# Attention operands turned by DMA instead of TensorE, and scores of two batches spread over two pairs of banks

## The chip, the cores and the metric

The kernel runs on one core of a Trainium2 chip. The core has TensorE (PE, matrix products and transposes into PSUM), VectorE (DVE), ScalarE (ACT), GpSimd (POOL) and SyncE (SP, which here only issues DMAs). Each engine works through its own list of instructions in order and waits on semaphores. The metric is device time in microseconds (us); three runs of the kernel before gave a median of 200.97 us (200.44 to 201.05). About 0.3% (0.6 us) is what such a measurement can tell from no change.

## The reference

The input x is 8 images of 16x16 positions with 128 channels, so 8 batches of 256 tokens. Three layers follow one another. Cut to what is computed:

```
# 1. self attention over positions (D = 16), all in float32
f, g, hh = xf @ Wf + bf, xf @ Wg + bg, xf @ Wh + bh
x = gamma * (softmax(f g^T) @ hh) @ Wv + bv + xf
# 2. t = t + attention_layer(layernorm(t)): 8 heads of 16
c = cos(h + theta); proj = cumprod(c) with column 0 = prod(c[1:])
ctx = softmax(proj proj^T / 4) @ proj          # queries = keys = values
x1 = layernorm(x + ctx @ W_comb.T + b_comb)
q = cos(x1[..., :8]) * cos(phi)
out = layernorm(x1 + relu(q @ W1.T + b1) @ W2.T + b2)
# 3. t = t + mixture(layernorm(t)): 32 experts of 32 hidden units, top 2
sel = top2(sigmoid(xt @ expert_sel.T))
out = sum over e of (relu(xt @ keys[e]) * w[e]) @ values[e]
```

## The kernel before

Every batch of 256 tokens (two tiles of 128) goes through some thirty steps: `conv_*` is layer 1, `proj_*` the cosines and running products of layer 2, `attn_*` its attention, `ffn_*` and `norm_second` the rest of it, `moe_*` layer 3. A step is a function with a batch number, and has a part on each engine that takes part. The order of the steps of all eight batches on one engine is written out by hand in the table `ORDER`: the eight numbers of a row are the places of that step for batches 0 to 7 in the engine's list, and `run_steps` calls the steps in that order. So batches overlap, and a step that waits holds up all that stands behind it on its engine. `warm` steps are places at which TensorE multiplies zeros (`keep_clock`, one 128x512 matmul each), which keep it at work where it would wait.

The steps that matter here, with their lines:

- `proj_split`: PA holds the 8 heads' 16 columns in float32. ScalarE casts them to fp16 (HL, high half, L781), VectorE takes the rest (low half, L1003), GpSimd writes the pair in swapped order into LH (L1228).
- `attn_transpose`: the scores need these with the 16 columns in partitions. TensorE turns eight 128x128 fp16 blocks (four of HL, four of LH) into one bank of the pair `sc_ps` (L579), and VectorE copies the bank to HLT (L1011). As the bank is that of the scores, this waits until ScalarE has taken the exponentials of the batch before.
- `attn_pair0` to `attn_pair3`: TensorE computes the scores of two heads (8 matmuls, L593) into the two banks of `sc_ps`; ScalarE takes the exponential of both banks in one instruction (L788). There is one pair of banks, so the scores of a pair wait for the exponential of the pair before.
- `attn_context` (L605), `attn_turn` (L613), `attn_back` (L620), `attn_combine` (L628): weighted sums, normalization by VectorE in between, output projection.
- `ffn_norm`, `ffn_cos`, `ffn_transpose`, `ffn_hidden` (L647, L808), `ffn_output` (L656), `moe_transpose` (XTT, L814), `moe_select`, and then `moe_pair` (L705 and L688), which is half of TensorE's work of a batch.
- On SyncE: the loads at the start, then per batch `moe_spread` (a 32 KB store to DRAM, L455), `moe_rows` (four loads of 256 KB that spread rows over partitions, L462) and `store` (L467).

Each of `conv_project`, `conv_stack`, `conv_scores`, `conv_turn` and `conv_output` works in `conv_ps`, for batches 1 and 3 in `hidden_ps[0]`.

Of the kernel before, what the change touches and what calls it, by code (L numbers as in the profile page):

```python
# [14 lines left out]
P = 128  # L15
# [40 lines left out]
        "moe_output": (137, 179, 202, 223, 246, 261, 268, 280),  # L56
        "warm": (1, 4, 6, 7, 9, 10, 11, 13, 15, 23, 24, 25, 26, 27, 28, 29, 31, 32, 33, 34, 38, 39, 42, 44, 45, 46, 47, 48, 52, 53, 55, 56, 57, 67, 72, 78, 79, 80, 83, 86, 101, 103, 104, 237, 238, 239, 241, 243, 244, 251, 255, 256, 258, 264, 270, 271, 272, 273, 274, 275, 276),
    },
    "scalar": {
        "conv_project": (0, 2, 11, 15, 24, 59, 79, 101),  # L60
        "prep_sel": (1,),
        "conv_scores": (3, 5, 13, 25, 46, 65, 87, 111),
        "conv_turn": (4, 7, 17, 30, 48, 67, 89, 114),
        "prep_keys": (6, 14),
        "sin_table": (8, 19, 34, 51, 72, 91, 117, 127, 145),
        "proj_cos": (9, 20, 36, 52, 74, 92, 97, 128),
        "prep_phi": (10,),
        "proj_split": (12, 22, 40, 56, 78, 96, 106, 131),
# [77 lines left out]
def build(nc, x, xT, pv, pa, pb, w2T, keys, values, out):  # L146
# [11 lines left out]
    with ExitStack() as es:  # L158
# [255 lines left out]
        def conv_bank(b):  # L414
            return hidden_ps[0] if b in (1, 3) else conv_ps
# [905 lines left out]
```

## Time and profile before

| | |
|---|---|
| median of three runs | 200.97 us |
| profiled execution | 200.5 us, of which its span 198.7 us |
| TensorE busy | 182.8 us (92%) |
| VectorE busy | 129.8 us (65%) |
| ScalarE busy | 109.6 us (55%) |
| GpSimd busy | 92.1 us (46%) |

Busy time of TensorE counts the multiplications by zeros. The span is what the profile shows of the execution; 1.8 us of it lie outside. A row of the timeline gives start, length and count of neighbouring like instructions; the lengths of matmuls are modelled and overlap, so the time that a group takes of TensorE is read from start to start.

### The profile page before, as it was taken

The numbers are of one execution on the slowest core, as the hardware profiler recorded it, in microseconds if no ns is written. First come the engines' busy times: TensorE is split into PE (matmuls) and PEld (weight loads), VectorE is DVE, ScalarE is ACT, GpSimd is POOL, SyncE is SP. The second block draws the span as 40 slices with busy tenths as digits, with TensorE's granted clock in tenths as the row PEclk, the third lists the DMA queues.
The fourth block names the chain that finished last, engine by engine and source line by source line (L and its number), as shares of the span: only waits on it lengthen the run. The fifth ranks groups of instructions, "written<-read, shape, count | busy, mean of one in ns | idle before, by whom it ended". The sixth has DMA issues, their size and how long they took to land.

```text
span 198.7 us, 4200 instructions
## 1 busy us (share of the span) xinstructions
PE 182.8 (92%) x1401; PEld 130.1 (65%) x1409; DVE 129.8 (65%) x451; ACT 109.6 (55%) x224; POOL 92.1 (46%) x237
## 2 busy tenths in 40 slices
PE   7999788888988899999999999999999968999994
PEld 3646445463755677776875786968777836766672
DVE  1166795447877578987996688686775753574332
ACT  2126598697988576597479689737815122010000
POOL 5734797846366862664494625542451540110000
PEclk9999999999999999999999999999999987999999
DMA  6990000000000450009001800720280090733600
GB/s 169 336 320 1 0 7 0 3 2 0 3 0 0 112 111 0 3 33 214 0 3 28 193 2 3 177 41 3 61 185 3 16 218 18 201 66 112 157 5 26
DMA packets 7174, 14.08 MB, mean 71 GB/s; under 512 B 1120, under 2 KB 5616, under 8 KB 6128
## 3 DMA queue, kind: packets, MB, share of 16 engines
q1 hardware_dynamic: 6848, 13.65, 26.2%
q8 instruction: 11, 0.18, 0.4%
q10 hardware_dynamic: 304, 0.16, 0.3%
q14 instruction: 11, 0.09, 0.2%
HBM read 12.49 MB, written 1.31 MB: 69 GB/s over the span
## 4 chain that ended last, share of the span: by engine, by line
PE 59%; POOL 12%; DVE 11%; ACT 7%; issue 5%; DMA 3%; SPq 1%; POOLq 0%; DVEq 0%; ACTq 0%
PE hidden_ps L705 12%; PE moe_ps L688 11%; PE sc_ps L593 6%; PE ffn_ps L656 6%; PE attn_ps L605 4%; PE hidden_ps L480 3%; PE conv_ps L561 3%; DMA pb_sb<-in_pb 3%; POOL rstd L1151 3%; ACT EB_ L788 2%; PE attn_ps L628 2%; PE ffn_ps L647 2%; PE attn_ps L613 2%; DVE HWT L1099 1%; PE sc_ps L579 1%
## 5 line engine op out<-in xcount | busy, mean ns | idle before, releaser
L788 ACT ACTIVATE EB_<-sc_ps 128x1024 f32<-128x1024 f32 x32 | 32.7, 1023 | 6.0 <-PE sc_ps L593 5.8
L705 PE MATMUL hidden_ps<-XTT,keys_sb 128*128 128x256 f32 x128 | 34.7, 394 | 0.0
L688 PE MATMUL moe_ps<-HWT,val_sb 128*128 128x256 f32 x128 | 34.1, 392 | 0.0
L1099 DVE SCALAR_TENSOR_TENSOR HWT<-hidden_ps,WB 128x512 f32<-128x512 f32 x32 | 21.9, 683 | 15.1 <-PE hidden_ps L705 13.3
L688 PEld LDWEIGHTS moe_ps<-HWT,val_sb 128*128 128x128 f32 x128 | 24.2, 194 | 4.2 <-DVE HWT L1099 1.0
L705 PEld LDWEIGHTS hidden_ps<-XTT,keys_sb 128*128 128x128 f32 x128 | 22.6, 193 | 4.8 <-DVE HWT L1099 2.0
L480 PE MATMUL hidden_ps<-idle_sb 128*128 128x512 bf16 x59 | 20.1, 435 | 2.9 <-DVE idle_sb L865 1.2
L1149 POOL TENSOR_SCALAR var<-mv 128x2 f32<-128x2 f32 x24 | 5.0, 207 | 36.6 <-DVE mv L874 36.0
L593 PE MATMUL sc_ps<-HLT 32*128 32x256 f16 x256 | 19.5, 270 | 2.4 <-ACT EB_ L788 1.8
L1151 POOL TENSOR_TENSOR rstd<-var,minushalf 128x2 f32<-128x2 f32 x24 | 16.8, 701 | 2.0
L593 PEld LDWEIGHTS sc_ps<-HLT 32*128 32x128 f16 x256 | 10.2, 92 | 11.2 <-issue 6.7
L605 PE MATMUL attn_ps<-EB_,PA 128*32 128x256 f32 x256 | 16.5, 384 | 0.0
L656 PE MATMUL ffn_ps<-w2T_sb,HID 128*128 128x128 f32 x128 | 15.9, 277 | 0.0
L656 PEld LDWEIGHTS ffn_ps<-w2T_sb,HID 128*128 128x128 f32 x128 | 15.2, 192 | 0.8 <-issue 0.4
L808 ACT ACTIVATE HID<-ffn_ps 128x512 f32<-128x512 f32 x16 | 9.5, 593 | 7.0 <-PE ffn_ps L647 7.0
L480 PEld LDWEIGHTS hidden_ps<-idle_sb 128*128 128x128 bf16 x67 | 6.8, 109 | 7.9 <-issue 2.2
L814 ACT COPY XTT<-ffn_ps 128x256 f32<-128x256 f32 x8 | 3.0, 372 | 16.1 <-PE ffn_ps L663 16.1
L768 ACT ACT_TABLE_LOAD x9 | 11.5, 1283 | 0.2
L1240 POOL TENSOR_TENSOR X1B<-X,b_b 128x256 f32<-128x256 f32 x8 | 5.8, 729 | 10.6 <-DVE X L1031 10.6
L605 PEld LDWEIGHTS attn_ps<-EB_,PA 128*32 128x32 f32 x256 | 7.0, 109 | 5.5 <-issue 1.3
L788 ACT ACT_TABLE_LOAD x7 | 9.0, 1283 | 0.1
L1031 DVE SCALAR_TENSOR_TENSOR X<-Z,rstd,pb_sb 128x128 f32<-128x128 f32 x16 | 4.9, 347 | 5.2 <-POOL rstd L1234 5.2
(173 smaller groups left out, 356.3 us busy)
## 6 DMA issues: line engine op xcount, KB each, us to landing
WB<-w_dram SPq DMA_DIRECT2D x32, 256.0 KB, 4.5
XT<-in_xT SPq DMA_DIRECT2D x8, 128.0 KB, 4.9
out<-OB SPq DMA_DIRECT2D x8, 128.0 KB, 1.8
X<-in_x SPq DMA_DIRECT2D x7, 128.0 KB, 5.0
keys_raw<-in_keys SPq DMA_DIRECT2D x1, 512.0 KB, 5.8
val_sb<-in_values SPq DMA_DIRECT2D x1, 512.0 KB, 6.4
pb_sb<-in_pb SPq DMA_DIRECT2D x1, 464.0 KB, 5.1
w2T_sb<-in_w2T SPq DMA_DIRECT2D x1, 256.0 KB, 5.0
```

Source lines behind the costliest of these rows:

```text
L480: mm(bank[:, :], idle_sb[:, 0:P], idle_sb[:, :], start=True, stop=True)
L561: last = mm(conv_bank(b)[:, t * (C + 1):(t + 1) * (C + 1)], ETs[:, b % 2, m, t * P:(t + 1) * P], HW[:, b % 2, m, :], start=(m == 0), stop= ...
L593: last = mm(sc_ps[i][:, t * N:(t + 1) * N], HLT[j, 0, h // 4, t * P:(t + 1) * P], HLT[j, side, h // 4, :], start=(side == 0), stop=(side = ...
L605: last = mm(attn_ps[32 * j:32 * j + 32, g * N:(g + 1) * N], PA[:, b % 2, t, h, :], EB_[:, h, t, :], start=(t == 0), stop=(t == TB - 1))
L656: last = mm(ffn_ps[:, t * C:(t + 1) * C], HID[:, k, t * P:(t + 1) * P], w2T_sb[:, k, :], start=(k == 0), stop=(k == FB - 1))
L688: last = mm(moe_ps[:, 0:N], val_sb[:, k, :], HWT[:, k % 4, :], start=(k == 0), stop=(k == EB - 1), skip_group_check=True)
L705: last = mm(hidden_ps[0][:, i * N:(i + 1) * N], keys_sb[:, k * EPB:(k + 1) * EPB, :].rearrange("p e h -> p (e h)"), XTT[:, b % 4, :], star ...
L768: fn(turned[:, i:i + 1], minushalf[:, 0:1], ACT.Silu)
L788: fn(EB_[:, 2 * p:2 * p + 2, :, :].rearrange("p h t n -> p (h t n)"), both_ps[:, :], ACT.Exp, scale=1.0 / math.sqrt(DK)).then_inc(s_prob, 1)
L808: fn(HID[:, 2 * half:2 * half + 2, :].rearrange("p k n -> p (k n)"), ffn_ps[:, :], ACT.Relu).then_inc(s_hid, 1)
L1099: V.scalar_tensor_tensor(out=HWT[:, half, :].rearrange("p i n -> p (i n)"), in0=hidden_ps[0][:, :], scalar=0.0, in1=WB[:, b % 2, 2 * q:2 * ...
L1151: G.tensor_tensor(rstd[:, which, b, :], var[:, which, b, :], minushalf[:, :], ALU.pow).then_inc(rs, 1)
```

## The change

1. `attn_transpose` leaves TensorE and VectorE. SyncE waits for HL and LH and issues eight DMA transposes of 128x128 fp16 from SBUF to SBUF. HLT is doubled, one half for each parity of the batch, with a semaphore for each parity and group of four heads: pairs 0 and 1 wait for group 0 (the first four DMAs), pairs 2 and 3 for group 1 (the last four).
2. For batches 0 and 1 the odd pairs put their scores into the two banks of `hidden_ps`, and the even ones into `sc_ps`, so a pair waits for the exponential of the pair before the last. The mixture, which uses `hidden_ps` too, waits for the eight exponentials of these batches.
3. `conv_project` of batch 0 is split: f and g first, which wait only for their inputs; the product for h goes to `attn_ps` once the folded weight is there. `prep_sel`, `prep_keys` and `prep_w1` use `attn_ps` and `ffn_ps`, and batches 1 and 3 of layer 1 use `moe_ps`.
4. `ffn_norm`: Z has a 129th column with a constant, and the squares are scaled, so the mean of squares plus epsilon comes out of the sum; one GpSimd instruction of two falls away.
5. `warm`: none between `prep_w1` and pair 3 of batch 1 (the 22 places in between issue nothing).
6. All five lists of `ORDER` are new.

```
 "sync": {
-    "moe_spread": (0, 2, 5, 7, 9, 12, 15, 19),
+    "attn_transpose": (0, 1, 2, 3, 6, 9, 11, 17),
+    "moe_spread": (4, 7, 12, 14, 18, 22, 25, 27),
...
-    HLT = sb("HLT", [P, 2, H // 4, N], F16)
+    HLT = sb("HLT", [P, 2, 2, H // 4, N], F16)
...
+    def spare(b, p):
+        return b < DOUBLE and p % 2 == 1
+    def score_bank(b, p):
+        return spare_ps if spare(b, p) else both_ps
...
+    def attn_transpose(b):                       # SyncE
+        sp.wait_ge(s_hi, b + 1)
+        sp.wait_ge(s_lo, b + 1)
+        if b >= 2:
+            sp.wait_ge(s_score_ps, H * (b - 1))
+        sp.wait_ge(s_lohi, b + 1)
+        for g in range(H // 4):
+            for side in range(2):
+                for t in range(TB):
+                    four = (HL, LH)[side][:, b % 2, t, 4 * g:4 * g + 4].rearrange("p h i d -> p (h i d)")
+                    sp.dma_start_transpose(HLT[:, b % 2, side, g, t * P:(t + 1) * P], four).then_inc(hlt_in[b % 2][g], 16)
...
     def warm(i):
-        if turned:
-            pe.wait_ge(s_wT, turned)
-        keep_clock(hidden_ps[1], 1)
+        if done("attn_pair3") >= DOUBLE:
+            pe.wait_ge(s_prob, H // 2 * DOUBLE)
+            if done("moe_spread"):
+                pe.wait_ge(s_wT, done("moe_spread"))
+            keep_clock(hidden_ps[1], 1)
+        elif not done("prep_w1"):
+            keep_clock(ffn_ps, 1)
...
     def conv_project(b):                         # TensorE
         if b == 0:
             pe.wait_ge(pa_in, 16)
+            for t in range(TB):
+                last = mm(conv_bank(b)[:, t * (2 * D + C):t * (2 * D + C) + 2 * D], XT[:, b, t * P:(t + 1) * P],
+                          wproj[:, 0:2 * D], start=True, stop=True)
+            last.then_inc(s_proj_ps, 1)
             pe.wait_ge(s_wproj_sb, 1)
+            for t in range(TB):
+                last = mm(attn_ps[:, t * C:(t + 1) * C], XT[:, b, t * P:(t + 1) * P], wproj[:, 2 * D:2 * D + C], ...)
...
-    def attn_transpose(b):                       # TensorE
...
-                    last = tr(b16(sc_ps[0], F16)[:, at:at + P], four, identh[:, :])
     def attn_pair(b, p):
-        pe.wait_ge(s_HLT, b + 1)
-        n = H // 2 * b + p
-        if n:
-            pe.wait_ge(s_prob, n)
+        pe.wait_ge(hlt_in[b % 2][p // 2], 64 * (b // 2 + 1))
+        if exps_before(b, p):
+            pe.wait_ge(s_prob, exps_before(b, p))
...
     def moe_pair(b, q):
         if b == 0 and q == 0:
+            pe.wait_ge(s_prob, H // 2 * DOUBLE)
...
     def ffn_norm(b):                             # GpSimd
-        G.tensor_scalar(var[:, 1, b, :], zsq[:, b, :], 1.0 / C, EPS, ALU.mult, ALU.add).then_inc(s_z_var, 1)
-        pool.wait_ge(s_z_var, b + 1)
-        G.tensor_tensor(rstd[:, 1, b, :], var[:, 1, b, :], minushalf[:, :], ALU.pow).then_inc(s_z_rstd, 1)
+        G.tensor_tensor(rstd[:, 1, b, :], zsq[:, b, :], minushalf[:, :], ALU.pow).then_inc(s_z_rstd, 1)
```

TensorE, from the two turns of batch 0 to its last scores (`conv_ps`, `moe_ps` and `hidden_ps` with FGp, FGT and EA are layer 1 of batches 2 to 4). Before:

```order
L543 MATMUL conv_ps<-FGT 128x256 x2
L524 MATMUL hidden_ps<-pa_sb,XT 128x160 x2
L579 MATMUL sc_ps<-identh,HL 128x128 x4
L579 MATMUL sc_ps<-identh,LH 128x128 x4
L480 MATMUL hidden_ps<-idle_sb 128x512 x2
L593 MATMUL sc_ps<-HLT 128x256 x8
L551 MATMUL conv_ps<-ident,EA 128x128 x4
L480 MATMUL hidden_ps<-idle_sb 128x512
L593 MATMUL sc_ps<-HLT 128x256 x8
L480 MATMUL hidden_ps<-idle_sb 128x512 x5
L593 MATMUL sc_ps<-HLT 128x256 x8
L561 MATMUL conv_ps<-HW,ETs 128x129 x4
```

The same place now:

```order
L583 MATMUL conv_ps<-FGT 128x256 x2
L591 MATMUL conv_ps<-ident,EA 128x128 x4
L576 MATMUL moe_ps<-identb,FGp 128x128 x4
L617 MATMUL sc_ps<-HLT 128x256 x8
L601 MATMUL conv_ps<-HW,ETs 128x129 x4
L617 MATMUL hidden_ps<-HLT 128x256 x8
L583 MATMUL moe_ps<-FGT 128x256 x2
L617 MATMUL sc_ps<-HLT 128x256 x8
L563 MATMUL conv_ps<-pa_sb,XT 128x160 x2
L617 MATMUL hidden_ps<-HLT 128x256 x8
L631 MATMUL attn_ps<-EB_,PA 32x256 x16
```

The turns and the multiplications by zeros are gone, the scores alternate between two pairs of banks, and both contexts of batch 0 follow at once. Behind them now stand the scores of batch 1, with `attn_back` (L646) and `attn_combine` (L654) of batch 0 among them:

```order
L639 MATMUL attn_ps<-ident,CT 128x128 x4
L617 MATMUL sc_ps<-HLT 128x256 x8
L617 MATMUL hidden_ps<-HLT 128x256 x8
L646 MATMUL attn_ps<-ident,CX 128x128 x2
L617 MATMUL sc_ps<-HLT 128x256 x8
L654 MATMUL attn_ps<-wcT_sb,CXT 128x128 x2
L617 MATMUL hidden_ps<-HLT 128x256 x8
```

`attn_combine` of batch 0 stands behind pair 2 of batch 1, the first that needs the last four transposes of that batch. ScalarE, from the cast of batch 0 (L812) to its first exponential of scores (L819), now:

```order
L812 CAST HL<-PA 128x16x16
L785 COPY HW<-moe_ps 128x2x128
L792 ACT_TABLE_LOAD
L792 ACTIVATE EA<-conv_ps,nmx 128x256 x2
L798 ACT_TABLE_LOAD
L798 ACTIVATE turned<-minushalf 128x1
L804 ACTIVATE CS<-ARG 128x256
L858 COPY ETs<-conv_ps 128x512
L819 ACT_TABLE_LOAD
L819 ACTIVATE EB_<-sc_ps 128x1024
L812 CAST HL<-PA 128x16x16
```

Before, a copy of keys stood there too, and of the loads of tables only one; the cast of batch 1 stood behind three exponentials of batch 0, and now stands behind one.

## Rows read from the trace of the kernel before

**Rows 1.** The page, busy time of each engine
```profile
PE 182.8 (92%) x1401; PEld 130.1 (65%) x1409; DVE 129.8 (65%) x451; ACT 109.6 (55%) x224; POOL 92.1 (46%) x237
```
**Rows 2.** Stretches: PE, PEld, DVE, ACT, POOL busy (instructions), clock, DMA share, GB/s
```profile
20.00:30.00 10.00, 7.89 (x64) 4.29 (x63) 7.96 (x27) 7.62 (x13) 8.58 (x19) 1.00 0.01 3
90.00:100.00 10.00, 10.00 (x96) 7.71 (x91) 8.80 (x35) 5.70 (x10) 5.39 (x11) 1.00 0.40 87
```
**Rows 3.** Turns and copy of batch 2, timeline of TensorE; the copies together
```profile
50.00 0.39 PE L579 MATMUL sc_ps<-identh,HL 128*128 128x128 f16 x4
50.23 0.39 PE L579 MATMUL sc_ps<-identh,LH 128*128 128x128 f16 x4
50.46 0.39 PE L543 MATMUL conv_ps<-FGT 128*128 128x256 bf16 x2
...
L1011 DVE COPY HLT<-sc_ps x8: 683/692/692, 24.6 to 129.5; 128x1024 f16<-128x1024 f16 x8
```
**Rows 4.** Timeline of the start, TensorE, VectorE and GpSimd
```profile
5.17 1.41 PE L524 MATMUL conv_ps<-pa_sb,XT 128*128 128x160 f32 x4
...
6.62 0.23 DVE L925 TENSOR_TENSOR FGs<-conv_ps,pa_sb 128x64 f32<-128x64 f32 x1 [1.17 <-PE conv_ps L524]
20.80 0.69 DVE L998 TENSOR_TENSOR_SCAN SC<-scanmask,CS 128x256 f32<-128x256 f32 x1 [0.48 <-ACT CS L774]
...
20.83 1.18 POOL L1176 TENSOR_TENSOR XR<-X,rc 128x256 f32<-128x256 f32 x1
21.97 0.62 POOL L1220 TENSOR_TENSOR PA<-SC,CS 128x240 f32<-128x240 f32 x1
...
23.70 0.40 POOL L1228 COPY LH<-HL 128x256 uint32<-128x256 uint32 x1 [0.96 <-DVE HL L1003]
```
**Rows 5.** The page, DMA issues; and SyncE's timeline
```profile
WB<-w_dram SPq DMA_DIRECT2D x32, 256.0 KB, 4.5
w_dram<-WT SPq DMA_DIRECT2D x8, 32.0 KB, 1.4
...
108.22 3.00 SPq L462 DMA_DIRECT2D WB<-w_dram  x4
123.54 0.30 SPq L455 DMA_DIRECT2D w_dram<-WT  x1
```
**Rows 6.** Timeline of ScalarE, the first exponentials and casts
```profile
22.77 0.41 ACT L781 CAST HL<-PA 128x256 f16<-128x256 f32 x1 [1.65 <-POOL PA L1221]
23.20 1.28 ACT L762 ACT_TABLE_LOAD   x1
24.49 0.84 ACT L762 ACTIVATE EA<-conv_ps,nmx 128x256 f32<-128x256 f32 x2
...
26.02 1.02 ACT L788 ACTIVATE EB_<-sc_ps 128x1024 f32<-128x1024 f32 x1
```
**Rows 7.** Timeline of TensorE, batch 0: last context, combine; first mixture product
```profile
35.95 1.07 PE L605 MATMUL attn_ps<-EB_,PA 128*32 128x256 f32 x16
36.96 0.61 PE L593 MATMUL sc_ps<-HLT 32*128 32x256 f16 x8
...
41.20 0.71 PE L628 MATMUL attn_ps<-wcT_sb,CXT 128*128 128x128 f32 x4
...
62.02 1.10 PE L705 MATMUL hidden_ps<-XTT,keys_sb 128*128 128x256 f32 x4
```
**Rows 8.** Stretches of 1 us, columns as in rows 2; timeline of two like groups
```profile
161.00:162.00 1.00, 0.75 (x6) 0.57 (x6) 0.75 (x3) 0.28 (x1) 0.65 (x2) 1.00 1.17 246
163.00:164.00 1.00, 1.00 (x5) 0.82 (x4) 0.44 (x4) 0.37 (x1) 0.00 (x0) 0.50 1.00 205
...
157.81 1.03 PE L688 MATMUL moe_ps<-HWT,val_sb 128*128 128x256 f32 x4
163.01 2.02 PE L688 MATMUL moe_ps<-HWT,val_sb 128*128 128x256 f32 x4
```
**Rows 9.** Instructions that write HL, with first and last start
```profile
L781 ACT CAST HL<-PA x8: 396/404/405, 22.8 to 127.4; 128x256 f16<-128x256 f32 x8
```

More of the change, by code:

```diff
@@ new lines @@
+        "conv_stack": (3, 10, 27, 47, 79, 111, 138, 163),
+        "conv_scores": (6, 13, 30, 51, 83, 114, 141, 166),
+        "conv_turn": (12, 17, 40, 57, 91, 119, 144, 174),
+        "prep_sel": (14,),
+        "conv_output": (15, 21, 49, 66, 94, 122, 147, 180),
+        "prep_keys": (16, 20),
[7 rows of a table added]
+        "attn_turn": (58, 75, 112, 131, 159, 179, 199, 220),
+        "attn_back": (61, 80, 117, 134, 161, 183, 204, 223),
+        "attn_combine": (64, 82, 120, 139, 164, 185, 207, 225),
+        "ffn_transpose": (76, 106, 130, 158, 186, 205, 224, 240),
@@ new lines @@
+        "prep_phi": (1,),
+        "conv_stack": (3, 5, 15, 22, 41, 57, 81, 105),
+        "conv_scores": (4, 6, 18, 27, 44, 60, 84, 109),
+        "conv_output": (7, 12, 23, 33, 51, 66, 90, 117),
+        "proj_norm": (8, 14, 25, 35, 56, 69, 96, 118),
+        "proj_angle": (10, 19, 30, 40, 59, 79, 98, 123),
+        "proj_reduce": (11, 20, 32, 43, 61, 80, 99, 125),
+        "proj_cos": (13, 21, 37, 47, 71, 85, 102, 128),
+        "proj_split": (17, 24, 39, 50, 75, 93, 104, 131),
+        "prep_attn": (28,),
@@ L131 @@
+        "moe_rows": (5, 8, 13, 16, 19, 23, 26, 29),
+        "store": (10, 15, 20, 21, 24, 28, 30, 31),
     },
@@ L225, in build @@
         s_lohi = sem("s_lohi")
-        s_HLT_ps = sem("s_HLT_ps")
-        s_HLT = sem("s_HLT")
+        hlt_in = [[sem(f"hlt_in{i}{g}") for g in range(2)] for i in range(2)]
         s_score_ps = sem("s_score_ps")
@@ L410, in build, with exps_before @@
         ffn_ps = ps("ffn_ps")
-        hidden_ps = [ps("hidden0_ps"), ps("hidden1_ps")]
+        spare_ps = es.enter_context(nc.psum_tensor("hidden_ps", [P, 4 * N], F32))
+        hidden_ps = [spare_ps[:, 0:2 * N], spare_ps[:, 2 * N:4 * N]]
         moe_ps = ps("moe_ps")
         def conv_bank(b):
-            return hidden_ps[0] if b in (1, 3) else conv_ps
+            return moe_ps if b in (1, 3) else conv_ps
+        DOUBLE = 2
+        def spare(b, p):
+            return b < DOUBLE and p % 2 == 1
+        def score_bank(b, p):
+            return spare_ps if spare(b, p) else both_ps
+        def exps_before(b, p):
+            n = H // 2 * b + p
+            return next((m + 1 for m in range(n - 1, -1, -1) if spare(m // 4, m % 4) == spare(b, p)), 0)
         def b16(bank, dt=BF16):
@@ L482, in warm, with done @@
             def warm(i):
-                at = ORDER["tensor"]["warm"][i]
-                turned = sum(p < at for p in ORDER["tensor"]["moe_spread"])
-                if turned:
-                    pe.wait_ge(s_wT, turned)
-                keep_clock(hidden_ps[1], 1)
+                order = ORDER["tensor"]
+                at = order["warm"][i]
+                def done(step):
+                    return sum(p < at for p in order[step])
+                if done("attn_pair3") >= DOUBLE:
[5 more added lines that the diff above has]
+                    keep_clock(ffn_ps, 1)
             pe.wait_ge(s_idle_set, 1)
@@ L599, in attn_context @@
                 pe.wait_ge(s_prob, H // 2 * b + 2 * g + 2)
+                if g == 0 and b == 0:
+                    pe.wait_ge(s_kc, 2)
                 if g == 0 and b:
@@ L766, in sin_table @@
                 if i == 0:
[L767 removed]
+                    act.wait_ge(s_ones_set, 5)
                 fn(turned[:, i:i + 1], minushalf[:, 0:1], ACT.Silu)
```

215 lines of the change are left out of this document (92 added, 123 removed), and 38 rows, old and new, of the table ORDER.

## The prediction

> **What bounds the kernel now.** I read the page's busy times first: TensorE 182.8 of 198.7 us, the next engine 129.8 [rows 1]. Then the stretches. From 62 to 158 us TensorE is as good as always busy (90 to 100 us: 10.00 of 10) while VectorE has 8.80; from 20 to 30 us it has 7.89, part of it products with zeros, and GpSimd 8.58 [rows 2]. So there are two regimes. Until the first mixture product at 62.02 [rows 7] a chain of latencies decides: batch 0 goes through layers 1 and 2 step by step. After it, work on TensorE decides: what is taken off it there, or what of it is done earlier, shortens the run. The last forty microseconds mix both. Last I read what stands around batch 0's attention on each engine, since both of the large edits act there.
>
> **The sum.** It is made against the profiled execution: 198.7 us of span and 1.8 outside. The median of the runs shown is 200.97, so 0.47 above that execution; I carry the difference over to it.
>
> *Turns off TensorE.* Four turns take 0.23 us from start to start (50.00, 50.23, 50.46), the eight of a batch 0.46, all eight batches 3.7 us; VectorE loses eight copies of 0.69, 5.5 us [rows 3]. The five batches behind 62 us, 5 x 0.46 = 2.3 us, count in full, since TensorE is saturated there. The three ahead of it lie in the chain and are counted there. VectorE's 5.5 us I take at nothing: behind 62 us it has over one microsecond in ten to spare, and TensorE hides the copy. If that cover went, they would be a gain too.
>
> *Start of the chain.* FGs of batch 0 is written at 6.62, behind four modelled matmul parts of 1.41 us that start at 5.17 with the folded weight [rows 4]. The new product of f and g is a fifth as wide and need not wait for the weight; I take 1.3 us. Further on, the running product SC is ready at 21.49 (20.80 + 0.69), but PA starts at 21.97, behind an XR of 1.18 us on GpSimd [rows 4]; XR of batch 1 now stands earlier, so 0.5 us more. LH of batch 0 ends at 24.10 before (23.70 + 0.40), and now at 22.3.
>
> *The DMA transposes.* No row shows one. Nearest by size is the store of WT, also 32 KB: 1.4 us from issue to landing. SyncE issues a DMA in 0.30 us (that store) to 0.75 (3.00 for four loads); loads of 256 KB land in 4.5 us [rows 5]. Bounds: fully overlapped, four are there after 3 x 0.30 + 1.4 = 2.3 us and eight after 3.5; one after the other, 5.6 and 11.2; one after the other at the loads' 4.5, 18 and 36, which is 288 us for the run and which I keep only as the far end. It cannot be a gain in itself, as LH must be ready first. I take issue at 0.75 and a landing of 1.4: 3.7 us for a group of four, 6.7 for eight. Batch 0's group 0 is then there at 26.0, against first scores at 25.3 before. Those DMAs meet no loads (0.01 DMA share from 20 to 30 us [rows 2]).
>
> *First exponential.* It was at 26.02. ScalarE's cast now ends at 21.4 (22.77 + 0.41 - 1.8), and then its list holds, by the lengths in [rows 6] and of like instructions, 0.4 (copy), three loads of tables of 1.28, 0.84 (EA), 0.6 (sine and its dummy), 0.6 (copy): 6.2 us, so 27.6. ScalarE, not the DMA, sets this: 1.6 us later than before.
>
> *Two pairs of banks.* Before, exponential, scores and table loads took turns, and the last context of batch 0 ended at 36.96 [rows 7], 10.9 us behind the first exponential. Now the exponentials follow one another: 27.6 + 4 x 1.02 + 0.4 for the cast between them + 1.1 for the context = 33.2. That is 3.8 us earlier.
>
> *The clock.* From that I take 2.0 us back. At 161 to 162 us TensorE is busy 0.75 of a microsecond, in a stretch of gaps; at 163 its granted clock is 0.50, the 1.2 GHz level, and the same four products take 2.02 instead of 1.03 us [rows 8]. The change takes the multiplications by zeros away from about 12 us to pair 3 of batch 1. Between 19 and 27 us TensorE then has a projection, three sets of turns of layer 1 and one product, under 2 us of work in 8. So I expect 1.2 GHz when the scores of batch 0 begin; `conv_output` of batch 2 stands between pairs 0 and 1 and doubles from 1 to 2 us, and the pair itself grows by 0.5, the context by 0.5. Bounds: 0, if the clock holds, and 4, if it stays low through batch 1. The last context of batch 0: 1.8 us earlier. The Trainium skill (TensorE: Matmul & The Clock Gate, "What's actually happening") puts it as the throttled state being the default that only activity lifts, which speaks against edit 5; the trace agrees with the 0.50 at 163 us, and without that rule nothing in the sum changes.
>
> *Combine of batch 0.* It was at 41.20 [rows 7], now 39.4, if it is not held. Ahead of it stands pair 2 of batch 1, which waits for all eight transposes of batch 1. Their cast follows the first exponential, at 28.6; LH is ready 1.3 us after a cast begins (22.77 to 24.10), at 29.9; eight transposes later it is 36.6. So it is not held; what is queued behind this wait is the combine, and with it everything of batch 0, which is why this is the sensitive place.
>
> *To the first mixture product.* In between, `ffn_output` no longer stands behind a pair (1.1 us of start time) and the variance step is gone (0.27): 3.2 us earlier altogether, at 58.8 instead of 62.02. Ahead of 62.02 stood a context (1.0), one more pair (0.6) and a turn (0.2) that now come behind it: +1.8. Warm steps behind that point: four more at the start, three fewer at the end, +0.2. Turns: -2.3.
>
> Sum: -3.2 + 1.8 + 0.2 - 2.3 = -3.5. The profiled execution would be 197.0 with a span of 195.2; the median 197.5, and I say 197.4 for the small savings of the last norm.
>
> *In steady state* a cast follows the one before after 14.9 us on average ((127.4 - 22.8) / 7) [rows 9]. Eight transposes in 6.7 us fit beside 2 us of other issues on SyncE, and HLT has two halves. Their cost there is nothing as long as some 7 us lie between LH and the first scores, which the new list leaves with seven or more steps of ScalarE (about 1.1 us each) in most batches.
>
> **Rivals.** Let p be the time of a transpose if only one is under way. LH of batch 1 is then at 25.2 + 4p, its eight are there at 25.2 + 12p, and the combine of batch 0 at 25.8 + 12p.
>
> 1. *One at a time, p = 1.4, as the 32 KB store lands.* Combine at 42.6, 1.4 later than before, first mixture product level with before. Sum 0.0 + 1.8 + 0.2 - 2.3 = -0.3: 200.7. For it: same size, and HL, LH and HLT have short rows of 256 bytes. Against it: four loads of 256 KB are issued within 3.00 us while each takes 4.5, so loads overlap [rows 5]. The Trainium skill (VectorE: DVE Perf Modes, "The three transpose paths") gives 1309 ns for a 128x128 DMA transpose against 390 ns on TensorE, and advises TensorE where PSUM will do; by its figure p = 1.31, an estimate of 199.6 us. No row here shows a DMA transpose, while TensorE's rows show 0.057 us each in a row of four.
> 2. *Slower: the transposes hold the combine for longer, p = 1.8.* Combine at 47.4, 6.2 later; 1.4 saved behind it, then -0.3: +4.5 us, 205.5. It decides from p = 1.4 on, and each further tenth costs 1.2 us here; from p = 1.9 (14.9 / 8) SyncE can't keep up in any batch. For it: nothing in this trace bounds p from above but 4.5. Against it: a 32 KB store through DRAM takes 1.4.
> 3. *The clock holds, or is back at once, and issue is 0.30.* Another 2 us: 195.4, and with SyncE always ahead the later batches' scores never wait: 194.5.
> 4. *The change does not do what it says:* the work behind 62 us is not saturated after the shift, because layer 1 or the norms come too late, so that only the turns count: 198.7. It lies within the forecast's own range.
>
> **How the numbers follow.** Forecast with rival 4, 196 to 199.6: 0.45. Rival 3, 193 to 196: 0.20. Rival 1, 199.6 to 202: 0.17. Rival 2, over 202: 0.15, two thirds of it within 206. The rest, 0.03, is below 193. Against 200.97, within 0.3% is 200.4 to 201.6: 0.09, nearly all from rival 1. Faster: 0.45 + 0.20 + 0.03 and 0.06 of rival 1, 0.74. Slower 0.17. The range takes in rivals 1 and 3 and the lower part of 2: 193.5 to 203.5; the likeliest case alone is 196 to 199.6.
>
> **What would show it.** SyncE's timeline: eight transposes of batch 0 from 22.3 us, 0.75 or less apart, each landing in about 1.4. First exponential at 27.6, last context of batch 0 by 35.2, combine at 39.4, first mixture product near 58.8. Granted clock 0.50 somewhere between 20 and 35 us, and full afterwards. TensorE busy over 9.5 of 10 from 60 to 155 us, with 64 turns fewer. Wrong would be: `attn_pair` waiting for HLT's DMAs by microseconds in batch 1 (rivals 1 and 2) or in later batches; clock losses behind 60 us; or gaps on TensorE between 60 and 150 us that wait for VectorE or GpSimd.

## The result: 233.63 us, and the profile after

The changed kernel takes 233.63 us (median of 4 runs, 233.46 to 235.95), the kernel before 200.7 on the same chip (199.47 to 201.05). The ratio is 1.168, 95% interval 1.159 to 1.177. The forecast was 197.4 with a range of 193.5 to 203.5: wrong in sign and by 36 us. The profiled run has a span of 231.3 us at a mean granted clock of 0.882. Some executions of a kernel lie over 1.5% above its fastest one; the medians given here count them, the ratios leave them out.

The experiments that matter most stand beside it. Those without transposes compute wrong scores and show only a time.

| kernel | median us | ratio to before, 95% |
|---|---|---|
| before | 200.7 | |
| the change | 233.6 | 1.168 (1.159 to 1.177) |
| no transposes at all | 199.8 | 1.000 (0.996 to 1.004) |
| no transposes, zeros back | 196.3 | 0.984 (0.980 to 0.989) |
| two wide transposes a batch, zeros back | 198.3 | 0.992 (0.988 to 0.996) |

The page of the changed kernel: busy times [rows 1], then the shares of the chain that ended last, by engine and by line, then its DMA issues [rows 5].

```profile
PE 191.4 (83%) x1330; PEld 133.4 (58%) x1330; DVE 125.7 (54%) x443; ACT 111.9 (48%) x226; POOL 90.9 (39%) x230
...
PE 34%; SPq 19%; DMA 13%; issue 11%; POOL 10%; DVE 8%; ACT 4%; POOLq 0%; DVEq 0%; ACTq 0%
SPq L472 17%; PE hidden_ps L731 8%; PE moe_ps L714 7%; DMA HLT<-LH 6%; DMA WB<-w_dram 4%; PE sc_ps L617 4%; PE attn_ps L631 3%; PE ffn_ps L682 2%; POOL rstd L1179 2%; PE hidden_ps L503 2%; DMA pa_sb<-in_pa 2%; SPq L485 1%; PE ffn_ps L697 1%; DMA w_dram<-WT 1%; POOL YB L1238 1%
...
WB<-w_dram SPq DMA_DIRECT2D x32, 256.0 KB, 4.3
...
HLT<-HL SPq DMA_TRANSPOSE x32, 2.3
HLT<-LH SPq DMA_TRANSPOSE x32, 2.4
```

L472 is the DMA transpose. SyncE's queue, which computes nothing, now carries 17% of the critical chain with it, and the landing of HLT another 6%. TensorE is busy for 8.6 us more although it has 71 matmul instructions fewer: the same work at a lower clock.

All transposes together, from the view of that line (duration min/median/max in ns, first and last start), and SyncE's timeline of batches 0 and 1:

```profile
L472 SPq DMA_TRANSPOSE HLT<-HL x32: 1093/1232/2112, 22.5 to 164.1; - x32
L472 SPq DMA_TRANSPOSE HLT<-LH x32: 1225/1232/2471, 25.0 to 166.6; - x32
```
```profile
22.49 2.44 SPq L472 DMA_TRANSPOSE HLT<-HL  x2
24.98 2.51 SPq L472 DMA_TRANSPOSE HLT<-LH  x2
27.53 2.51 SPq L472 DMA_TRANSPOSE HLT<-HL  x2
30.08 2.51 SPq L472 DMA_TRANSPOSE HLT<-LH  x2
33.49 2.37 SPq L472 DMA_TRANSPOSE HLT<-HL  x2
```

Each holds the queue for 1.23 us in the median; eight take 10 us, and the landing is 2.3 to 2.4 us behind the issue, not 1.4 as for the store of WT. Sixty-four are 79 us of SyncE's time.

TensorE's timeline at batch 0's attention [rows 7], and the stretches with it (columns as in rows 2):

```profile
28.63 1.03 PE L617 MATMUL sc_ps<-HLT 32*128 32x256 f16 x8 [1.95 <-DMA HLT<-LH]
...
34.78 1.03 PE L617 MATMUL sc_ps<-HLT 32*128 32x256 f16 x8 [1.59 <-DMA HLT<-LH]
...
38.08 3.63 PE L631 MATMUL attn_ps<-EB_,PA 128*32 128x256 f32 x32
...
45.40 0.71 PE L654 MATMUL attn_ps<-wcT_sb,CXT 128*128 128x128 f32 x4
...
69.98 1.91 PE L731 MATMUL hidden_ps<-XTT,keys_sb 128*128 128x256 f32 x4
```
```profile
20.00:30.00 10.00, 4.41 (x28) 2.56 (x28) 5.33 (x16) 6.72 (x11) 6.89 (x16) 0.55 0.09 18
30.00:40.00 10.00, 8.41 (x58) 4.83 (x61) 4.37 (x18) 4.85 (x7) 2.12 (x4) 0.50 0.13 27
...
60.00:70.00 10.00, 8.26 (x49) 6.11 (x50) 3.52 (x12) 5.40 (x7) 3.57 (x8) 0.60 0.12 24
...
140.00:150.00 10.00, 5.22 (x19) 3.38 (x20) 4.50 (x18) 1.01 (x6) 0.95 (x2) 0.53 0.26 56
```

Both groups of HLT are waited for, and from the first wait to 40 us the work is done at the 1.2 GHz level (0.50). Behind the later long waits the clock falls again: 0.60 from 60 to 70 us, 0.53 from 140 to 150. The waits by line (sum, times, longest):

```profile
ACT EB_ L819 <- PE sc_ps L617: 18.1, 16, 3.2
PEld sc_ps L617 <- DMA HLT<-LH: 17.6, 9, 3.5
...
PE sc_ps L617 <- DMA HLT<-LH: 14.2, 8, 3.3
```

These eight waits fall into six batches, twice into batches 0 and 2, never into 1 and 3. That is not all of it. The longest single stall of TensorE waits for HWT, the mixture's product with the weights WB. TensorE and SyncE, 120 to 145 us:

```profile
144.78 2.08 PE L731 MATMUL hidden_ps<-XTT,keys_sb 128*128 128x256 f32 x4 [6.18 <-DVE HWT L1126]
```
```profile
131.77 3.75 SPq L472 DMA_TRANSPOSE HLT<-LH  x2
135.62 0.51 SPq L478 DMA_DIRECT2D w_dram<-WT  x1
137.30 1.71 SPq L485 DMA_DIRECT2D WB<-w_dram  x4
```

ScalarE had written WT of batch 2 at 127.7 us. Its store went out at 135.6, since SyncE was issuing transposes from 112.5 on without a pause but for one store, and WB's four loads land some 4.3 us behind their issue. The store of batch 1 was 6.9 us late in the same way (written at 95.6, issued at 102.5); from batch 3 on the stores go out at once. So two theories stood from here on. **Distance**: HLT comes later behind LH than the order allows, in most batches. **Blocking**: the transposes hold SyncE's queue, and what stands behind them, WT's store and WB's loads, comes late. A third, **clock**: both are small, and the 1.2 GHz level does the rest.

### The profile page after: what moved, and what is told of

It reads as the page before. It is cut to its first block, busy times and chain, and to the rows that moved or that the text cites. A ratio compares the mean times of both kernels' runs of the same rounds, so it can differ in the third digit from the quotient of the medians.

```text
span 231.3 us, 4122 instructions
## 1 busy us (share of the span) xinstructions
PE 191.4 (83%) x1330; PEld 133.4 (58%) x1330; DVE 125.7 (54%) x443; ACT 111.9 (48%) x226; POOL 90.9 (39%) x230
## 4 chain that ended last, share of the span: by engine, by line
PE 34%; SPq 19%; DMA 13%; issue 11%; POOL 10%; DVE 8%; ACT 4%; POOLq 0%; DVEq 0%; ACTq 0%
SPq L472 17%; PE hidden_ps L731 8%; PE moe_ps L714 7%; DMA HLT<-LH 6%; DMA WB<-w_dram 4%; PE sc_ps L617 4%; PE attn_ps L631 3%; PE ffn_ps L682 2%; POOL rstd L1179 2%; PE hidden_ps L503 2%; DMA pa_sb<-in_pa 2%; SPq L485 1%; PE ffn_ps L697 1%; DMA w_dram<-WT 1%; POOL YB L1238 1%
## 5 line engine op out<-in xcount | busy, mean ns | idle before, releaser
L731 PE MATMUL hidden_ps<-XTT,keys_sb 128*128 128x256 f32 x128 | 38.1, 424 | 7.3 <-DVE HWT L1126 7.3
L819 ACT ACTIVATE EB_<-sc_ps 128x1024 f32<-128x1024 f32 x28 | 28.7, 1024 | 18.2 <-PE sc_ps L617 18.1
L714 PE MATMUL moe_ps<-HWT,val_sb 128*128 128x256 f32 x128 | 35.9, 408 | 0.0
L617 PE MATMUL sc_ps<-HLT 32*128 32x256 f16 x224 | 20.1, 306 | 15.3 <-DMA HLT<-LH 14.2
L731 PEld LDWEIGHTS hidden_ps<-XTT,keys_sb 128*128 128x128 f32 x128 | 24.2, 207 | 13.5 <-DVE HWT L1126 9.6
L1261 POOL TENSOR_TENSOR rstd<-zsq,minushalf 128x2 f32<-128x2 f32 x8 | 5.9, 741 | 35.6 <-ACT ZQ L865 35.6
L631 PE MATMUL attn_ps<-EB_,PA 128*32 128x256 f32 x256 | 18.2, 415 | 0.3 <-ACT EB_ L819 0.3
L682 PE MATMUL ffn_ps<-w2T_sb,HID 128*128 128x128 f32 x128 | 17.1, 290 | 0.0
L503 PE MATMUL hidden_ps<-idle_sb 128*128 128x512 bf16 x41 | 12.9, 423 | 2.4 <-ACT WT L878 1.3
L1257 POOL COPY LH<-HL 128x256 uint32<-128x256 uint32 x8 | 3.2, 400 | 16.1 <-DVE HL L1036 16.1
L845 ACT COPY XTT<-ffn_ps 128x256 f32<-128x256 f32 x8 | 3.0, 372 | 12.6 <-PE ffn_ps L689 12.6
L1238 POOL TENSOR_TENSOR YB<-Y,bcc_b 128x256 f32<-128x256 f32 x8 | 6.4, 798 | 5.8 <-DVE bcc_b L988 4.8
```

The costliest lines, as they stand in the source:

```text
L503: mm(bank[:, :], idle_sb[:, 0:P], idle_sb[:, :], start=True, stop=True)
L617: last = mm(score_bank(b, p)[:, (2 * i + t) * N:(2 * i + t + 1) * N], HLT[j, b % 2, 0, h // 4, t * P:(t + 1) * P], HLT[j, b % 2, side, h / ...
L631: last = mm(attn_ps[32 * j:32 * j + 32, g * N:(g + 1) * N], PA[:, b % 2, t, h, :], EB_[:, h, t, :], start=(t == 0), stop=(t == TB - 1))
L682: last = mm(ffn_ps[:, t * C:(t + 1) * C], HID[:, k, t * P:(t + 1) * P], w2T_sb[:, k, :], start=(k == 0), stop=(k == FB - 1))
L714: last = mm(moe_ps[:, 0:N], val_sb[:, k, :], HWT[:, k % 4, :], start=(k == 0), stop=(k == EB - 1), skip_group_check=True)
L731: last = mm(hidden_ps[0][:, i * N:(i + 1) * N], keys_sb[:, k * EPB:(k + 1) * EPB, :].rearrange("p e h -> p (e h)"), XTT[:, b % 4, :], star ...
```

## The experiments

### What the change would give with free transposes

Without any transpose (HLT is set to zero once, so all scores are zero; they wait for HL and LH only):

```diff
-                sp.dma_start_transpose(HLT[...], four).then_inc(hlt_in[b % 2][g], 16)
-                pe.wait_ge(hlt_in[b % 2][p // 2], 64 * (b // 2 + 1))
+                pe.wait_ge(s_lohi, b + 1)
```

> The changed kernel with no DMA transpose at all: HLT is set to zero once at the start, so the scores are zero, and the scores wait only for LH. Everything else (order, two pairs of banks, few multiplications by zeros) stays. If the DMA transposes and what waits for them are the whole loss, this runs about as the prediction had it with a free transpose: 193 to 197 us, with a granted clock of 0.97 or more from 40 us on. If the new order or the missing multiplications by zeros cost time by themselves, it stays over 203 us, with clock losses between 60 and 180 us.

Measured: 199.79 us (10 runs), ratio 1.000 (0.996 to 1.004), between the two expected answers (193 to 197, over 203). The transposes are the loss of 34 us, but taking them away leaves no gain either. From 20 to 40 us the clock is low:

```profile
20.00:30.00 10.00, 5.85 (x34) 4.22 (x34) 5.83 (x17) 8.32 (x14) 6.89 (x16) 0.68 0.01 2
30.00:40.00 10.00, 9.82 (x88) 4.97 (x86) 5.01 (x20) 5.64 (x10) 4.92 (x13) 0.64 0.00 1
```

So the same, with the products of zeros back in the 22 warm places that the change leaves empty early on (into `ffn_ps`, and `prep_w1`'s copy on ScalarE earlier so that the bank is free):

```diff
-                elif not done("prep_w1"):
-                    keep_clock(ffn_ps, 1)
+                else:
+                    if done("prep_w1"):
+                        pe.wait_ge(s_w1T, 1)
+                    keep_clock(ffn_ps, 1)
```

> The kernel without any DMA transpose (HLT set to zero once) with its 22 silent warm places used, into ffn_ps. Without them it ran at 1.00 of the kernel before, with a clock of 0.66 from 20 to 40 us and the combine of batch 0 at 41.7 us. If the clock ate the gain of the start, the clock is 0.9 or more there, the combine comes at 39.5 and the run takes 195.5 to 198.5 us. If the start is bound by ScalarE and GpSimd whatever the clock, the combine comes at 41 or later and the run stays within 1 us of 199.5.

Measured: 196.25 us (4 runs), ratio 0.984 (0.980 to 0.989), and the clock is up:

```profile
20.00:30.00 10.00, 8.61 (x59) 5.00 (x61) 6.25 (x18) 7.83 (x13) 6.63 (x16) 1.00 0.01 2
30.00:40.00 10.00, 9.18 (x112) 5.30 (x109) 6.45 (x24) 8.98 (x16) 6.31 (x16) 1.00 0.01 2
```

The empty places cost 3.5 us (the rows: 0.68 and 0.64 become 1.00). Is the clock then what the change lacks? The same edit on the changed kernel itself:

> The changed kernel with its 22 silent warm places used (a multiplication by zeros into ffn_ps once ScalarE has copied the turned W1, which it does earlier). If the clock that fell at 21 us is a cause, the granted clock stays at 1.00 until the first scores, the last context of batch 0 ends about 3 us earlier (42 to 39) and the run gains 2 to 4 us of 33. If the clock is only a consequence of waiting for the DMAs, the run gains under 1.5 us. That the clock explains most of the loss would show as a gain over 10 us.

Measured: 235.06 us (2 runs), ratio 1.178 (1.167 to 1.190): nothing gained. TensorE still waits 15.5 us for HLT. So the clock at the start is not the cause of the 33 us; the falls behind the later waits remain in this run, as its waits do.

### Number and shape of the transposes

Four narrow ones a batch, HL alone (the second product reads HL's half again, so LH's share of the scores is wrong):

```diff
-                    for side in range(2):
+                    for side in range(1):
```

> Four DMA transposes a batch instead of eight: only the blocks of HL are turned, and the second matmul of each score reads the turned HL again instead of LH (same matmuls, other numbers). If each DMA costs its 1.23 us of SyncE and the loss is linear in them, the time lies halfway between the changed kernel and the one without transposes, near 214 us. If there is a point from which it hurts (the distance between LH and the first scores, some 7 us, against 4 x 1.23 + 2.4 = 7.3), most of the loss is gone: under 205 us. If a fixed latency is what hurts, over 224 us.

Measured: 202.8 us (2 runs), ratio 1.016 (1.005 to 1.028). TensorE hardly waits for HLT (0.6 us, two weight loads). From four to eight costs 31 us, the first four 3: something is used up in between.

All of the data in two instructions, 128 rows by 512 columns each (HLT laid out [side, t, g, 128]; all pairs wait for both):

```diff
-                for g in range(H // 4):
-                    for side in range(2):
-                        for t in range(TB):
...
-                            sp.dma_start_transpose(HLT[:, b % 2, side, g, t * P:(t + 1) * P], four)...
+                for side in range(2):
+                    both = (HL, LH)[side][:, b % 2].rearrange("p t h i d -> p (t h i d)")
+                    sp.dma_start_transpose(HLT[:, b % 2, side].rearrange("p t g n -> p (t g) n"), both)...
```

> The changed kernel with two DMA transposes a batch instead of eight, each of 128 rows by 512 columns (four blocks), into an HLT laid out by tile and group; all four pairs wait for both. If SyncE's 1.23 us are paid per instruction, the two take about 2.5 us and land some 3 us later: no wait of the scores beyond the first batches and 199 to 204 us. If they are paid per block, each takes about 4.9 us, the batch takes the same 10 us, pair 0 waits for all of it instead of half, and the run is as slow as the changed kernel or slower: 233 to 245 us.

Measured: 200.1 us (8 runs), ratio 1.002 (0.997 to 1.007), level with no transposes at all. Its SyncE timeline:

```profile
22.87 1.30 SPq L470 DMA_TRANSPOSE HLT<-HL  x1
24.22 1.26 SPq L470 DMA_TRANSPOSE HLT<-LH  x1
31.85 1.19 SPq L470 DMA_TRANSPOSE HLT<-HL  x1
33.08 1.27 SPq L470 DMA_TRANSPOSE HLT<-LH  x1
```

An instruction of four blocks holds the queue as long as one of a single block. The price is per instruction.

Four of 256 columns, between the two:

> Kernel: the change with four DMA transposes a batch in place of eight, each of 128 rows by 256 columns, so all of the data is moved; all pairs wait for the four. Theory (the price is paid per instruction): each occupies SyncE's queue for about 1.25 us as the narrow ones and the wide ones do, the last lands 4 x 1.25 + 2.3 = 7.3 us behind LH, and the time is that of the kernel with four narrow ones (202.8) or a little below: 200 to 204. Rival (the amount of data decides, and the four narrow ones were cheap since they moved half of it): over 208, or over 2 us of queue for an instruction.

Measured: 220.14 us (4 runs), ratio 1.102 (1.092 to 1.111). The expected 200 to 204 was missed. The time lies where the rival had it (over 208), but not for the rival's reason, the amount of data: these too take 1.25 us each, and two wide ones move as much in a run of 200.1 us. What I had overlooked is that in the kernel with four narrow ones pairs 0 and 1 wait for two of them, and here all pairs wait for four. HLT is whole 3 x 1.25 + 2.4 = 6.2 us behind LH (7.3 in the batches where a landing took longer), against 3.8 to 3.9 for two wide ones, and the waits on TensorE say so:

```profile
PE sc_ps L616 <- DMA HLT<-LH: 12.6, 5, 3.0
```
```profile
PE 184.9 (85%) x1330; PEld 129.9 (60%) x1330; DVE 125.9 (58%) x443; ACT 111.8 (52%) x226; POOL 90.9 (42%) x230
```

The second row is its page. With two wide ones the same 1330 matmul instructions keep TensorE busy for 179.0 us, so 5.9 us of the loss are the lower clock behind the waits. 12.6 + 5.9 = 18.5 us, and the spans differ by 18.7 (216.3 and 197.6).

Which batches wait? The time from LH's end to the batch's first scores, read from the timelines of GpSimd and TensorE:

| batch | 0 | 1 | 2 | 3 | 4 | 5 | 6 | 7 |
|---|---|---|---|---|---|---|---|---|
| no transposes | 4.2 | 7.1 | 4.0 | 8.0 | 4.3 | 4.5 | 5.6 | 4.2 |
| two wide | 4.2 | 7.0 | 4.0 | 8.0 | 4.3 | 4.5 | 5.6 | 4.8 |
| four of 256 columns | 7.3 | 7.0 | 6.3 | 10.8 | 7.3 | 6.3 | 6.4 | 7.2 |
| the change | 6.2 | 9.6 | 6.2 | 11.8 | 7.6 | 6.2 | 8.4 | 7.1 |

The first row is what the new order leaves: 4.0 to 4.5 us in five batches. Two wide transposes fit into it. With four, TensorE waits in just these five.

Narrow ones for batches 0 and 1, wide ones after:

> Kernel: eight narrow DMA transposes for batches 0 and 1 as in the change, two wide ones for batches 2 to 7. Theory 1 (the loss is made anew in each batch, 3 us or so at a time, as the lags of the first scores of 3.3, 6.1, 9.4, 12.0, 14.3, 17.6, 18.0 us show): only the lag of batches 0 and 1 is left, about 4 to 6 us over the wide kernel's 200.1: 203 to 207 us. Theory 2 (a late start throws the whole static order out of step, and the later batches only pay for it): most of the 31 us stay, over 218.

Measured: 207.02 us (4 runs), ratio 1.037 (1.030 to 1.043), 6.9 above two wide ones throughout. The loss is made anew from batch to batch, not handed down from a late start.

### The old order, and the turns back on TensorE

The kernel before with nothing changed but that the turns are DMA transposes, LH to scores as close as it was:

> The kernel before with only the turns moved: DMA transposes from SyncE, doubled HLT, and every other list of steps as before (multiplications by zeros included). The old order leaves about 1.3 us between LH and the first scores. If the distance to the scores is what counts, each batch waits some 10 us and the run takes 240 us or more, slower than the changed kernel. If the queue of SyncE is what counts, it loses what the changed kernel loses, 228 to 236 us. If the clock is what counts, it is faster than the changed kernel, since the zeros are back.

Measured: 264.77 us (2 runs), ratio 1.326 (1.318 to 1.335). Distance again, for the old list leaves least of it, 1.2 to 2.2 us in seven batches: TensorE waits 39.2 us for HLT in all, and 11.4 for HWT besides. The rest of the change, its order above all, had won 31 us of that back. And the new order with the turns on TensorE and VectorE's copy:

> The changed kernel with the turns back on TensorE and the copy back on VectorE, at new places in the new order; two pairs of banks, split first projection and few multiplications by zeros stay. If the DMA is what lost the time, this is level with the kernel before or better: 194 to 201 us (3.7 us of turns come back against the predicted 197). If the new order is bad by itself: over 205 us.

Measured: 203.42 us (4 runs), ratio 1.022 (1.013 to 1.030), between its two expected answers. With the zeros as well:

> Kernel: the order of the change and the zeros at the 22 places as well, but the turns on TensorE with VectorE's copy. It is the partner of the kernel with two wide DMA transposes and zeros. If moving the turns off TensorE is worth what the prediction took (2.3 us behind the first mixture product), it is 2 to 3 us above that one: 198.5 to 200.5 us. Rival: the turns on TensorE are hidden in its gaps and the wide transposes gain nothing: both within 0.8 us of each other.

Measured: 202.44 us (4 runs), ratio 1.011 (1.004 to 1.019), above the 198.5 to 200.5 that was expected. So the new order with the turns on TensorE is no gain over the kernel before. How much of that is the order, and how much the places that the turns were given in it, is open: no other places were tried.

### Distance and blocking, apart

First, WT's store and WB's loads issued by ScalarE's queue in place of SyncE's.

```diff
-            run_steps("sync", {..., "moe_spread": moe_spread, "moe_rows": moe_rows, "store": store})
+            run_steps("sync", {"attn_transpose": attn_transpose, "store": store})
...
+                act.wait_ge(w_out[b % 2], 16 * (b // 2 + 1))
...
+                    act.dma_start(WB[e * HE:(e + 1) * HE, b % 2]..., ...)
```

> The changed kernel with the weights' way to the mixture (the store of WT and the four loads of WB) issued by ScalarE instead of SyncE, the loads some steps behind the store; SyncE keeps the transposes and the stores of the output. If the transposes hurt most by standing ahead of those on SyncE's queue, the 6.2 us stall of the mixture at 138 to 144 us goes, with its consequences, and the run takes 214 to 224 us. If they hurt by the 10 us until the turned operands are there, it takes over 228 us.

Measured: 240.48 us (2 runs), ratio 1.205 (1.198 to 1.211), slower still. Read by its expectation, blocking would be small. But it is no clean test. The stall at 138 to 144 us did go: every store now leaves when WT is written. The loads are late instead, 4 to 10 us behind WT in batches 4 to 6 where 1.5 is usual, for their places in ScalarE's list stand behind other waits of ScalarE. Its timeline for batch 6:

```profile
200.51 0.31 ACTq L867 DMA_DIRECT2D w_dram<-WT  x1
210.22 0.31 ACTq L874 DMA_DIRECT2D WB<-w_dram  x1
```

TensorE waits 6.9 us for HWT in all (7.3 in the change), so blocking was moved and not removed, and 18.1 us for HLT (14.2).

Cleaner are six spare transposes of a constant into a buffer that nobody reads, behind the two wide ones:

```diff
+                sp.wait_ge(s_ident, 6)
+                for i in range(6):
+                    sp.dma_start_transpose(SPARE[:, 6 * (b % 2) + i], identh[:, :]).then_inc(s_spare, 16)
```

> Kernel: two wide DMA transposes a batch as before, and behind them in SyncE's queue six narrow ones of a constant identity into a spare buffer that nobody reads. SyncE's queue and the DMA engines carry eight instructions a batch as in the change, but HLT is there about 3.8 us behind LH. Latency theory (only the distance from LH to HLT counts): 200 to 204 us, a little over the wide kernel's 200.1 where the spare ones hold the loads of WB up. Rival (the transposes' time in the queue, or what they do to other DMAs, costs the 31 us): over 215 us.

Measured: 224.34 us (4 runs), ratio 1.120 (1.111 to 1.129). HLT is early, and 24 us are lost all the same, so distance alone (200 to 204 expected) does not explain the change. The waits of TensorE and VectorE, and SyncE at the first stall:

```profile
PE hidden_ps L734 <- DVE HWT L1128: 16.9, 5, 7.9
...
DVE HWT L1128 <- issue: 14.4, 2, 8.3
...
DVE HWT L1128 <- DMA WB<-w_dram: 8.5, 3, 5.2
...
PE sc_ps L620 <- DMA HLT<-LH: 0.4, 1, 0.4
```
```profile
64.34 7.61 SPq L475 DMA_TRANSPOSE SPARE<-identh  x6
72.00 0.58 SPq L481 DMA_DIRECT2D w_dram<-WT  x1
73.73 2.61 SPq L488 DMA_DIRECT2D WB<-w_dram  x4
```

Scores hardly wait (0.4 us); HWT does. "issue" means that the profile names no releaser; both such waits, 6.1 and 8.3 us, are at the first product of a batch with WB, and there are none in the kernels without WB's path below. The stores of WT go out 6.3, 6.0 and 9.1 us late in batches 0 to 2 and at once in the others, so the blocking is done in three batches. The same six ahead of the wide ones:

> Kernel: the same eight instructions a batch, but the six spare ones stand ahead of the two wide ones, behind the same waits for HL and LH. HLT is there 6 x 1.23 + 3.8 = 11.2 us behind LH, for all pairs. Latency theory, with a price of one microsecond a batch for each microsecond beyond 3.8, which fits the kernel of four wide of 256 columns (6.1 us, 220.1) and the one with only batches 0 and 1 narrow (207.0): 200.1 + 8 x 7.4 = 259, so 245 to 265 us. Rival (the work in the queue decides and not its place): as the kernel with the six behind, within 5 us.

Measured: 264.37 us (4 runs), ratio 1.321 (1.309 to 1.332), by the same instructions in another place. TensorE waits 49.3 us for HLT, in all eight batches, and is busy for 16.5 us more than with two wide ones (195.5 against 179.0) at the lower clock. So distance is real too. HLT comes 7.4 us later than there, and the loss is 64 us, 8.0 a batch on the mean: about one microsecond a batch for each microsecond, the clock included.

Last, WT's store and WB's loads left out, VectorE multiplying by four blocks of `val_sb` of the same shape (the weights of the mixture are missing from the result). First with the six spare ones behind:

```diff
-                    dve.wait_ge(wb_in[b % 2], 16 * EPB * (b // 2 + 1))
+                    dve.wait_ge(val_in, 16)
-                                       in1=WB[:, b % 2, 2 * q:2 * q + 2, :].rearrange("p i n -> p (i n)"),
+                                       in1=val_sb[:, 4 * (q % 2):4 * (q % 2) + 4, :].rearrange("p i n -> p (i n)"),
```

> Kernel: as the one with six spare transposes behind the two wide ones, but the store of WT and the loads of WB are left out, and VectorE multiplies by four blocks of val_sb of the same shape in place of WB (so the mixture's weights are left out of the result). Theory (the 24 us of the kernel with WB came from the store of WT and the loads of WB waiting in SyncE's queue behind the spare transposes: three waits of HWT of 5 to 8 us): the whole loss goes, 198 to 202 us, and HWT waits for no DMA. Rival (the spare transposes cost by themselves, by SBUF or the DMA engines or GpSimd's waits): over 215.

Measured: 201.32 us (10 runs), ratio 1.010 (1.005 to 1.015). 23.0 of the 24 us go with WB's path. What the kernel with two wide transposes alone would gain by leaving WB's path out was not run; HWT waits 3.1 us for WB in it. Leaving the path out also takes its loads off the DMA engines, so this run alone does not tell blocking in the queue from traffic; the late stores in the timelines above are what speaks for the queue. Then the changed kernel with the same part left out:

> Kernel: the change with its eight narrow transposes, and the same part left out (no store of WT, no loads of WB). It leaves the distance from LH to HLT and takes the blocking of WB away. Theory (in the change most waits of TensorE are for HLT, 14.2 us in sum, and one long one of 6.2 for HWT at 138.5 us): 221 to 228 us, that is 6 to 12 below the change, and the rest is distance. Rival 1 (the two are in series, and blocking is the main one): 205 to 214. Rival 2 (removing WB only makes TensorE come sooner to the same wait for HLT): 231 or more.

Measured: 219.1, 220.7, 225.1 and 226.2 us, median 222.91, and 219.9 for the two lower ones, which are the ones to compare; 221 to 228 was expected. What is left of the change without WB's path is distance:

```profile
PEld sc_ps L617 <- DMA HLT<-LH: 18.4, 10, 3.2
...
PE sc_ps L617 <- DMA HLT<-LH: 15.3, 10, 3.0
```

### The version that beats both

Two wide transposes and the zeros:

> Kernel: the order of the change, two DMA transposes a batch (128 rows by 512 columns each), and the 22 early warm places filled again with products of zeros. Latency theory: the two instructions put HLT in place about 2 x 1.25 + 2.3 = 4.8 us behind LH, which cost nothing against no transposes at all (200.1 against 199.8 us), and the zeros gave 3.5 us there (199.8 to 196.3). So 196 to 197.5 us, the granted clock 1.00 from 20 to 40 us and 0.98 or more on the mean. Rival: with the clock up TensorE comes to the scores sooner and waits for the transposes instead, so that the zeros bring under 1 us: 199 to 200.5, with waits for HLT's DMAs of over 3 us in sum.

Measured: 198.28 us (12 runs), ratio 0.992 (0.988 to 0.996): faster than the kernel before by 0.4 to 1.2%, while 196 to 197.5 was expected. The rival had part of it: with the clock up, scores wait for HLT for 1.9 us in all. Against its partner with turns on TensorE the wide DMA form is 3.8 us faster, by the two ratios (1.011 and 0.992).

## Why the prediction was wrong

**The step that failed** is "I take issue at 0.75 and a landing of 1.4". Measured: 1.23 and 2.3 to 2.4. Four are there after 6.1 us and eight after 11.2 where nothing holds them up, where I had 3.7 and 6.7. The nearest rows misled: a load or store of SyncE [rows 5] is another operation. My bounds "one after the other", 5.6 and 11.2 us, lay next to the truth, and I had chosen values well below them.

**The second** is "Their cost there is nothing as long as some 7 us lie between LH and the first scores, which the new list leaves". The condition was stated and not measured: I counted steps in the list and took 1.1 us for each. The new order leaves 4.0 to 4.5 us in five batches, and 7 or more only in batches 1 and 3 (the table above). HLT after 3.8 to 3.9 us costs nothing, after 6.2 it costs 20. In the kernel before it is 1.2 to 2.2 us in seven batches, which its trace shows and which speaks against a guess of 7. This step turned the sign, for the price recurred in six of eight batches; rivals 1 and 2 charged it once, at batch 0's combine. By rival 1's formula the measured 1.23 would have meant no loss. The signs of being wrong that the prediction named did appear: `attn_pair` waits for HLT in later batches, and the clock falls behind 60 us.

**The third** is missing altogether: who stands behind the transposes in SyncE's queue. The prediction set "Eight transposes in 6.7 us fit beside 2 us of other issues on SyncE" against 14.9 us, a sum of times, as if a queue with room in the mean could not make anything late. WT's store was 6.9 us late in batch 1 and 7.9 in batch 2, behind the transposes of batches 4 and 6, and for batch 2 TensorE stood still for 6.2 us.

**The clock** was named and undersized: 2.0 us were taken, 3.5 measured (199.8 with empty places, 196.3 with zeros). In the change itself each long wait brings another fall: TensorE is busy 191.4 us there and 179.0 in the kernel with two wide transposes, with the same 1330 matmul instructions. So some 12 of the 33.7 us between their spans are, by the modelled lengths of the matmuls, the same work at the lower clock, and only the rest is waiting itself. With HLT early it is gone: the granted clock is 0.963 with two wide transposes and 0.882 in the change.

**What was right.** Start of the chain: LH(0) ends at 22.39 (predicted 22.3); ScalarE is ready for the first exponential at 27.63 (27.6), though HLT, not ScalarE, then sets it, at 29.73. With free transposes and the clock up, the combine of batch 0 comes at 38.5 us and the first mixture product at 58.4, where 39.4 and 58.8 were forecast with 2 us taken for the clock. The value of the rest with free transposes: 196.25 at full clock, against rival 3's 195.4. That taking the turns off TensorE is worth 2.3 us or more fits, but is not shown by itself. Without transposes, `moe_transpose` of batch 0 begins at 59.0 (57.3 before) and that of batch 7 at 173.3 (174.1 before), 2.5 us gained between the two, but that stretch has other edits of the order too; the pair of kernels with wide transposes and with turns on TensorE differs by 3.8 us.

**The account**, from 197.4 to 233.6: 2.4 to the kernel without transposes (199.8: clock 1.5 more than taken, 0.9 other terms); 1.5 to the one with early HLT, spare transposes and no WB path (201.3); 18.6 by distance (219.9); 13.7 by blocking. With the median of all four runs of that kernel (222.9) the last two are 21.6 and 10.7. They also depend on the order in which they are taken: with HLT early, blocking alone costs 23.0 (201.3 to 224.3). Where HLT is late, WB's loads have more time, and part of the blocking is covered; I infer that from the two differences and have not shown it by itself. Left open is also why an instruction costs 1.23 us whatever its width; only its size was measured.

## What to carry to other kernels

Before work moves to a DMA queue, measure two distances in the trace, batch by batch: from the producer's end to the consumer's start, and from each other instruction of that queue to whoever waits for it; a mean load of the queue says nothing of either. When no row shows an operation, the bound that charges it one after the other is a value to calculate with, in every batch and not only where the chain looks tightest. And if a price is per instruction, widen the instruction: two in place of eight turned a loss of 33 us into none.

## What the runs showed of the hardware

- A DMA transpose of f16 from SBUF to SBUF holds SyncE's queue for 1.23 us (median of 64, up to 2.47) and lands 2.3 to 2.4 us after its issue (median, up to 4.1). Neither grows much with its width: 128 x 128, 128 x 256 and 128 x 512 held the queue for 1.23, 1.25 and 1.19 to 1.27 us and landed after 2.3, 2.4 and 2.5. The Trainium skill (VectorE: DVE Perf Modes, "The three transpose paths") gives 1309 ns for a 128x128 bf16 block. The trace comes near it as to the queue, 1.23; from issue to data it is nearly twice that. For the wide form the queue time is 0.32 us a block.
- In sequence they do not overlap in the queue: eight take eight times 1.23, 10 us. Their landings do overlap with the next issues: eight are there after 11.2 us, not after eight times 2.3.
- Six spare transposes a batch that nobody waits for cost little by themselves once nothing of use stood behind them in the queue: 201.3 us, a ratio of 1.010, against 200.1 and 1.002 with the two wide ones alone.
